# Four-layer graph network on one core: layer two's spread turns its quads through two PSUM banks, two ahead of the weighing, and keeps the scan's mask in SBUF

## Chip, cores and metric

One Trainium2 chip, one core. The metric is the device time of one execution in microseconds (us), outside the profiler; of the kernel before there are three runs.

## What is computed

Four message-passing layers over a graph with 12,500 nodes of 32 features and 400,000 edges sorted by their target; after each comes a residual and a layer norm. The change is in the second layer:

```
bu, bv = tent(edge_attr[:, 0], 4), tent(edge_attr[:, 1], 4)     # hat functions on 4 centres
basis = (bu[:, :, None] * bv[:, None, :]).reshape(-1, 16)
xj = x[edge_index[1]]
msg = sum_k basis[:, k:k+1] * (xj @ weight[k])                  # 16 matrices of 32 x 32
out = segment_sum(msg, edge_index[0], num_segments=n_nodes)
x = layernorm(x + out)
```

For this layer the kernel's source node is the one by which the edges are sorted (`edge_index[1]` is dst), so xj is constant over a run of edges, and the sum goes to scattered nodes.

## The kernel before

Edges lie as [128 partitions x 3125]; every edge stage walks them in 125 chunks of T = 25 columns. Chunk 0 is written out, the other 124 run in a loop of 31 turns with four chunks each (k = 1 to 4). The engines are programmed by hand: each has its own instruction list in the order of the code, and waits on semaphores. The stages, in order of time: layer 1 (chunks with gathers by GpSimd, L1957), its ends, **the spread** of layer 2 (`vector_spread`, `tensor_spread`, `scalar_spread`, `gpsimd_spread`, `sync_spread`), the fold of layer 2 (33 chunks), layer 3 (gathers L1979), layer 4 (gathers L1939).

The spread, one chunk c:
- SyncE loads the injected rows (`S1.inj`) and the edge coordinates (`S1.at`), four buffers each.
- ScalarE (`scalar_chunk1`) waits until the scatters of chunk c - 4 have landed (semaphore `sc{s4}`), copies 25 numbers into the payload buffer (L1340), lays out the scan's input (L1349) and the mask `S1.mr` (L1350), makes the tents (L1354, L1357), and then copies seven turned quads from PSUM to SBUF (`S1.xT`, two buffers, L1362).
- VectorE (`vector_chunk1`, 41 instructions) subtracts the centres (L695), carries the last column over (L697), and spreads the node rows over their runs by a scan with the mask (L700). It multiplies the rows by four tents (L665, two instructions, `oA` for columns 0 to 11 and `oB` for 12 to 24). Then five times a one-hot (L564, `row`) and a rank (L677 and L679, `rank`), and seven times a weighted sum (L688 and L691, `mix`), interleaved; seven small instructions (L723 to L734) make the scatter addresses, the last is `adr`.
- TensorE (`tensor_chunk1`) works on quads of four columns: `turn(g)` transposes four 128x128 blocks into a PSUM bank (L1668), `weigh(g)` multiplies the copied transposes by the weights into bank 2 or 3 (L1677), `before(q)` and `behind(q)` are the rank's triangular matmuls into banks 0 and 1 (L1651, L1652). `mix(g)` waits for `weigh(g)`, `rank(q)` for `before(q)`, `behind(q)` for the first half of `rank(q)`.
- GpSimd (`gpsimd_chunk1`) waits for `adr` and issues 25 indirect DMAs of one column each (L1900), which scatter the payload `S1.pay` (four buffers) to `pay_d`. VectorE's `mix(0)` of chunk c writes into the buffer that chunk c - 4 scattered, so VectorE may be up to about three chunks ahead of GpSimd.

Before the change all seven quads turn through one bank, `ps[6]`: `turn(g + 1)` stands behind `weigh(g)`, and has to wait until ScalarE has copied quad g out. The mask lies in PSUM banks 4 and 5 (`psall[:, 2048:2880]`). The scans of layers 1 and 3 (L847, L1009) also take their mask from PSUM; layer 4's scan (L1158) takes it from SBUF, written there by L1468.

Of the kernel before, what the change touches and what calls it, by code (L numbers as in the profile page):

```python
# [10 lines left out]
ACT = mybir.ActivationFunctionType  # L11
# [6 lines left out]
T = 25  # L18
# [24 lines left out]
def nth4(i, k):  # L43

    return i + 1 + k // 4
# [21 lines left out]
def gnn_kernel(nc, x, src, dst, ea2, ea3, ea5, ew, ew1, W0, W1, G2, MU, SG, ROOT, BIAS, w1, b1, w2, b2, out):  # L67

    ctx = ExitStack()
    with ctx:  # L70
        ctx.enter_context(nc.allow_non_contiguous_dma(reason="small strided loads of weights and block heads"))

        def sb(name, shape, dt=F32):
            return ctx.enter_context(nc.sbuf_tensor("s_" + name, shape, dt))
# [6 lines left out]
        def sem(name):  # L81
            if name not in sems:
                sems[name] = ctx.enter_context(nc.semaphore("m_" + name))
            return sems[name]
# [30 lines left out]
        ident = sb("ident", [P, P])  # L115
# [31 lines left out]
        psall = ctx.enter_context(nc.psum_tensor("psall", [P, 4096], F32))  # L147
        ps = [psall[:, 512 * i:512 * i + 512] for i in range(8)]
# [7 lines left out]
        def barrier(e, name):  # L156

            n = barriers[name] = barriers.get(name, 0) + 1
            e.drain().then_inc(sem("bar"), 1)  # L159
            e.wait_ge(sem("bar"), 5 * n)  # L160
            e.sem_inc(idle2 if name == "sync" else idle, 1)
# [17 lines left out]
        cv = Carve()  # L179
        dsti, dstf, q2 = cv(TP, I32), cv(TP), cv(TP)  # L180
        cv = Carve(17900)
# [12 lines left out]
        for layer in (0, 2):  # L194
            cv = Carve(15400 if layer == 0 else 0)
# [4 lines left out]
        cv = Carve(10350)  # L200
# [23 lines left out]
        cv = Carve()  # L224
# [12 lines left out]
        cv = Carve()  # L237
# [4 lines left out]
        S1 = Spread()  # L242
# [12 lines left out]
        S1.adr = [cv(T, U32) for _ in range(4)]  # L255
        S1.pq, S1.pi, S1.pa = cv(T), cv(T, I32), cv(T)
        S1.wt, S1.wl = cv(128), cv(128)
        assert cv.at <= TOP
        S1.tv = ps[7][:, 0:4 * T]
        S1.cen = ps[7][:, 200:204]  # L260
        S1.mr = psall[:, 2048:2048 + 32 * (T + 1)]
        S1.mrv = S1.mr.rearrange("p (f t) -> p f t", f=32)
        QUADS = [(4 * g, 4) for g in range(6)] + [(24, 1)]

# [1 line left out]
        cv = Carve()  # L266
# [19 lines left out]
        cv = Carve()  # L286
# [11 lines left out]
        cv = Carve(21400)  # L298
# [10 lines left out]
        cv = Carve()  # L309
# [22 lines left out]
        cv = Carve()  # L332
# [308 lines left out]
        def v1(c, name):  # L641

            return c * PER1 + (mk["base1"] + ST[name])
# [692 lines left out]
        def scalar_chunk1(e, c, i, k):  # L1336
            i_ = 0 if i is None else i
            s4, s2 = k % 4, k % 2
            e.wait_ge(sem(f"sc{s4}"), (0 if i is None else i * 400) + (416 if k == 4 else 16))
            e.activation(S1.pay[s4].rearrange("p (t c) -> p t c", c=33)[:, :, 32:33], lo[:, bass.ds(c * T, T)].unsqueeze(2), ACT.Copy).then_inc(sem("p1_lo"), 1)  # L1340
            e.wait_ge(sem(f"inj1_{s4}"), nth4(i_, k) * 16)
            e.wait_ge(dv.h, v1(c - 1, "scan"))
            if i is None:


                e.wait_ge(sem("ld_d0"), 16)
                e.activation(S1.siv[0][:, :, 1:2], frow[:, :].unsqueeze(2), ACT.Copy)
            t0 = 1 if i is None else 0
            e.activation(S1.siv[s2][:, :, 1 + t0:T + 1].rearrange("p f t -> p t f"), S1.inj[s4][:, 32 * t0:].rearrange("p (t f) -> p t f", f=32), ACT.Copy)  # L1349
            e.activation(S1.mrv[:, :, 1:T + 1], mask[:, bass.ds(c * T, T)].unsqueeze(1).to_broadcast([P, 32, T]), ACT.Copy).then_inc(sem("p1_si"), 1)  # L1350

            te = S1.tent.rearrange("p (t d m) -> p t d m", t=T, d=2)
            e.wait_ge(dv.h, v1(c, "tent"))
            e.activation(S1.tent, S1.tent, ACT.Abs).then_inc(sem("p1_a"), 1)  # L1354
            e.wait_ge(sem("p1_a"), c + 1)
            for d, o_ in ((1, S1.tv), (0, S1.tu)):
                e.activation(o_.rearrange("p (t m) -> p t m", t=T), te[:, :, d], ACT.Relu, scale=-1.0 / H3C, bias=ones[:, 0:1]).then_inc(sem("p1_b"), 1)  # L1357
            for g, (t0, n) in enumerate(QUADS):
                xb = (k + g) % 2
                e.wait_ge(sem("p1_t"), c * 7 + (g + 8))  # L1360
                e.wait_ge(sem("p1_y"), c * 7 + (g + 1))
                e.activation(S1.xT[xb][:, 0:128 * n], ps[6][:, 0:128 * n], ACT.Copy).then_inc(sem("p1_x"), 1)  # L1362

        def scalar_spread(e):
            e.sem_inc(sem("p1_b"), 2)
            e.sem_inc(sem("p1_si"), 4)
            e.sem_inc(sem("p1_x"), 1)
            e.wait_ge(sem("ld_wt1"), 64)
            e.activation(S1.wt.rearrange("p (o a) -> p o a", a=4), S1.wl.rearrange("p (a o) -> p o a", a=4), ACT.Copy).then_inc(sem("p1_w"), 1)
            barrier(e, "scalar")  # L1370
            scalar_chunk1(e, 0, None, 0)
            with e.Fori(0, 31) as i:
                for k in range(1, 5):
                    scalar_chunk1(e, i * 4 + k, i, k)
# [217 lines left out]
        def scalar_program(e):  # L1592
            scalar_setup(e)
            scalar_table(e, 0)
            scalar_ends(e)
            scalar_edges0(e)
            e.wait_ge(sem("ld_ew"), 32)
            scalar_ends_of(e, 0)
            scalar_spread(e)
            barrier(e, "scalar")  # L1600
            scalar_fold(e)
            scalar_ends_of(e, 1)
            scalar_table(e, 2)
            barrier(e, "scalar")
            scalar_edges2(e)
            scalar_ends_of(e, 2)
            scalar_edges3(e)
            scalar_ends_of(e, 3)
            barrier(e, "scalar")
# [40 lines left out]
        def both(e, lhsT, rhs, start):  # L1650
            e.matmul(R5s[:, 0:4], lhsT, rhs[:, 0:4], start=start, stop=True, skip_group_check=True)  # L1651
            return e.matmul(R5s[:, 4], lhsT, rhs[:, 4], start=start, stop=True, skip_group_check=True)  # L1652
# [8 lines left out]
        def tensor_chunk1(e, c, k):  # L1661
            def turn(g):

                t0, n = QUADS[g]
                e.wait_ge(dv.h, v1(c, "oA" if t0 < 12 else "oB"))
                e.wait_ge(sem("p1_x"), c * 7 + (g + 1))
                for t in range(n):
                    m = e.transpose(ps[6][:, 128 * t:128 * t + 128], S1.xb[:, 128 * (t0 + t):128 * (t0 + t) + 128], ident[:, :])  # L1668
                m.then_inc(sem("p1_t"), 1)

            def weigh(g):
                t0, n = QUADS[g]
                yb = (k + g) % 2
                e.wait_ge(sem("p1_x"), c * 7 + (g + 2))
                e.wait_ge(dv.h, v1(c, f"mx{g - 2}") if g > 1 else v1(c - 1, f"mx{g + 5}"))
                for t in range(n):
                    m = e.matmul(ps[2 + yb][:, 128 * t:128 * t + 128], S1.xT[yb][:, 128 * t:128 * t + 128], S1.wt, start=True, stop=True)  # L1677
                m.then_inc(sem("p1_y"), 1)

            def before(q):  # L1680
                e.wait_ge(dv.h, v1(c, f"oh{q}"))
                both(e, trib, O[q], False).then_inc(sem("rk"), 1)

            def behind(q):
                e.wait_ge(dv.h, v1(c, f"tm{q}"))
                both(e, ntrib, O[q], False).then_inc(sem("rk"), 1)

            turn(0)
            before(0)
            for g in range(4):  # L1690
                weigh(g)
                turn(g + 1)
                behind(g)
                before(g + 1)
            weigh(4)
            turn(5)
            behind(4)
            weigh(5)
            turn(6)
            weigh(6)  # L1700

        def tensor_spread(e):
            e.sem_inc(sem("p1_t"), 7)
            e.sem_inc(sem("p1_y"), 2)
            barrier(e, "tensor")
            e.wait_ge(sem("p1_w"), 1)
            tensor_chunk1(e, 0, 0)
            with e.Fori(0, 31) as i:
                for k in range(1, 5):
                    tensor_chunk1(e, i * 4 + k, k)  # L1710
# [556 lines left out]
```

## Time and profile before

| | us |
|---|---|
| runs of the kernel before | 17419.0, 17419.1, 17439.26 |
| median | 17419.1 |
| span of the profiled execution | 22369.0 |
| layer 1's chunks in it (first to last gather L1957) | 202.2 to 4570.8 |
| the spread in it (first to last scatter L1900) | 4971.7 to 10827.7 |
| layer 3's chunks (L1979) | 11454.7 to 15800.7 |
| layer 4's chunks (L1939) | 15985.0 to 22107.1 |

The page gives no device time of the profiled execution other than its span, and that is 4950 us above the runs without the profiler. So the profile shows well how long single instructions take, while its waits have to be read with care: some of them are in the profiled execution alone. The granted clock is the mean of TensorE's clock, 0.5 being 1.2 GHz and 1.0 being 2.4 GHz.

### The profile page before, as it was taken

Reading aid. Unit: us, or ns where it says so; the run is one execution under the profiler, and the core shown is the slowest. Engines: PE = TensorE matmul, PEld = TensorE weight load, DVE = VectorE, ACT = ScalarE, POOL = GpSimd, SP = SyncE. Lnnn points to the kernel's source line nnn. Section 1 sums busy time; section 2 is a strip of 40 time slices with the busy share of each in tenths; the row PEclk is TensorE's granted clock in tenths of the full one; section 3 lists DMA queues with packets and bytes.
Section 4 is the critical chain, followed back from the end, with each engine's and each line's share of the span. In section 5 each row is a group of like instructions: output and inputs, shape, how many; then the busy total and the mean of one; then the engine's idle time right before and its main releaser. Section 6 shows DMA issues by size and latency. Waiting matters only on the chain. (4 is left out here: it accounts for less than half of the span.)

```text
span 22369.0 us, 139122 instructions
## 1 busy us (share of the span) xinstructions
PE 7326.9 (33%) x33487; PEld 5554.2 (25%) x33487; DVE 12331.2 (55%) x15713; ACT 3280.0 (15%) x5336; POOL 13220.2 (59%) x13715
## 2 busy tenths in 40 slices
PE   1000000014444444444420000000166666666665
PEld 0000000003333333333310000000155555555553
DVE  5566666646666666666742222222366666666665
ACT  0000000001111111111520000000011211211111
POOL 7766666655555555555667777777644444444444
PEclk9555555556666666666655555555588888888887
DMA  3232232210000000000322222222111111111111
GB/s 94 80 89 84 86 89 86 85 36 19 18 19 19 18 19 19 19 19 18 131 92 52 53 52 52 53 52 53 34 35 37 36 35 36 36 35 37 36 35 30
DMA packets 744245, 1076.69 MB, mean 48 GB/s; under 512 B 375704, under 2 KB 508494, under 8 KB 731295
## 3 DMA queue, kind: packets, MB, share of 16 engines
q0 software_dynamic: 417376, 477.82, 9.8%
q1 hardware_dynamic: 250851, 398.14, 6.3%
q10 hardware_dynamic: 75736, 197.70, 2.4%
q8 instruction: 88, 1.44, 0.0%
q14 instruction: 194, 1.58, 0.0%
HBM read 684.92 MB, written 389.48 MB: 48 GB/s over the span
## 5 line engine op out<-in xcount | busy, mean ns | idle before, releaser
L1939 POOL DMA_INDIRECT s_arena<-d_t,s_arena x3125 | 2963.9, 948 | 3178.4 <-DVE s_arena L1091 1107.9
L1900 POOL DMA_INDIRECT d_pay<-s_arena x3125 | 3029.2, 969 | 2873.4 <-DVE s_arena L697 1464.3
L1979 POOL DMA_INDIRECT s_arena<-d_t,s_arena x3125 | 3320.8, 1063 | 1106.6 <-issue 1026.1
L1957 POOL DMA_INDIRECT s_arena<-d_t,s_arena x3125 | 2993.1, 958 | 1405.8 <-issue 1373.3
L1758 PE MATMUL psall<-s_w2r,s_arena 128*128 128x384 f32 x4750 | 2107.2, 580 | 1550.1 <-DVE s_arena L1091 625.2
L1651 PE MATMUL psall<-s_arena 128*128 128x500 bf16 x1875 | 945.5, 559 | 4749.1 <-remote 2889.7
L992 DVE TENSOR_TENSOR s_arena<-s_arena,psall 128x2400 f32<-128x2400 f32 x125 | 332.0, 2656 | 3141.9 <-DMA s_arena<-d_t,s_arena 3141.9
L1677 PE MATMUL psall<-s_arena 128*128 128x128 f32 x6250 | 1356.1, 381 | 1813.2 <-ACT s_arena L1362 1706.9
L1758 PEld LDWEIGHTS psall<-s_w2r,s_arena 128*128 128x128 f32 x4750 | 1447.1, 320 | 1943.0 <-DVE s_arena L1091 687.6
L1677 PEld LDWEIGHTS psall<-s_arena 128*128 128x128 f32 x6250 | 1166.0, 277 | 2111.8 <-issue 1209.9
L1088 DVE TENSOR_TENSOR s_arena<-psall,s_arena 128x512 f32<-128x512 f32 x1000 | 786.7, 787 | 1454.1 <-remote 1161.2
L1651 PEld LDWEIGHTS psall<-s_arena 128*128 128x128 bf16 x1875 | 243.2, 130 | 5164.8 <-remote 2934.6
L901 DVE TENSOR_REDUCE s_arena<-s_arena 128x600 f32<-128x4200 f32 x125 | 1027.2, 8218 | 775.5 <-remote 678.6
L1840 PE MATMUL psall<-s_tails,s_mfix 128*128 128x32 f32 x6 | 1.9, 412 | 4400.9 <-POOLq L159 4374.3
L1100 DVE TENSOR_REDUCE s_arena<-s_arena 128x64 f32<-128x1024 f32 x1000 | 1397.6, 1408 | 0.2 <-issue 0.2
L1362 ACT ACTIVATE s_arena<-psall 128x512 f32<-128x512 f32 x875 | 482.9, 552 | 4807.9 <-remote 2507.1
L1668 PE MATMUL psall<-s_ident,s_arena 128*128 128x128 f32 x3125 | 719.6, 369 | 1274.9 <-DVE s_arena L665 1274.9
L688 DVE TENSOR_TENSOR s_arena<-psall,s_arena 128x512 f32<-128x512 f32 x875 | 550.6, 629 | 1056.2 <-remote 935.3
L1840 PEld LDWEIGHTS psall<-s_tails,s_mfix 128*128 128x128 f32 x6 | 1.5, 313 | 4402.6 <-issue 4374.6
L564 DVE TENSOR_TENSOR s_arena<-s_arena,psall 128x625 bf16<-128x625 f32 x1250 | 962.7, 801 | 132.8 <-issue 132.4
L677 DVE TENSOR_TENSOR s_arena<-s_arena,psall 128x625 f32<-128x625 bf16 x625 | 503.1, 805 | 938.3 <-remote 720.3
L1668 PEld LDWEIGHTS psall<-s_ident,s_arena 128*128 128x128 f32 x3125 | 554.8, 197 | 1298.1 <-issue 1298.1
(303 smaller groups left out, 16992.3 us busy)
## 6 DMA issues: line engine op xcount, KB each, us to landing
s_arena<-d_t,s_arena POOLq DMA_INDIRECT x9375
d_scan<-s_arena ACTq DMA_DIRECT2D x375, 400.0 KB
s_arena<-d_ew SPq DMA_DIRECT2D x126, 800.0 KB
s_arena<-d_pay SPq DMA_DIRECT2D x33, 1650.0 KB, 6.8
d_inj<-s_agg SPq DMA_DIRECT2D x125, 400.0 KB
s_arena<-d_inj SPq DMA_DIRECT2D x125, 400.0 KB
d_pay<-s_arena POOLq DMA_INDIRECT x3125
d_fold<-s_arena ACTq DMA_DIRECT2D x33, 1250.0 KB, 4.9
```

The source lines that it names most:

```text
L564: return e.tensor_tensor(O[sl], h5[:, :, bass.ds(n, 1)].to_broadcast([P, 5, 125]), iob, ALU.is_equal)
L901: e.tensor_reduce(S[:, :, 8:32], w7.rearrange("p m t c -> p t c m"), AX.X, ALU.add)
L1088: e.tensor_tensor(pr[:, :, 0:256].rearrange("p t (b v) -> p t b v", v=16), Rg[:, :, 0:256].rearrange("p t (b v) -> p t b v", v=16), L3.G[s ...
L1100: e.tensor_reduce(L3.sums[s2][:, t0:t0 + n].rearrange("p t c -> p (t c)"), prod(g).rearrange("p t (b v) -> p (t b) v", v=16), AX.X, ALU.ad ...
L1651: e.matmul(R5s[:, 0:4], lhsT, rhs[:, 0:4], start=start, stop=True, skip_group_check=True)
L1668: m = e.transpose(ps[6][:, 128 * t:128 * t + 128], S1.xb[:, 128 * (t0 + t):128 * (t0 + t) + 128], ident[:, :])
L1677: m = e.matmul(ps[2 + yb][:, 128 * t:128 * t + 128], S1.xT[yb][:, 128 * t:128 * t + 128], S1.wt, start=True, stop=True)
L1758: m = e.matmul(ps[BANK[g] + t][:, 0:384], hv_[:, :, t0 + t], L3.w2v if g in ONPE else w2r[:, :], start=True, stop=True)
L1900: e.indirect_dma_start(pay_d, bass.IndirectOffsetOnAxis(ap=S1.adr[s4][:, t:t + 1], axis=0), S1.pay[s4][:, 33 * t:33 * t + 33], None).then_ ...
L1939: e.indirect_dma_start(L3.gb[s][:, t], None, T3_d, bass.IndirectOffsetOnAxis(ap=L3.idx[s][:, t:t + 1], axis=0)).then_inc(sem(f"g3_{s}"), 16)
L1957: e.indirect_dma_start(L0.gb[s][:, t * 128:(t + 1) * 128], None, T0_d, bass.IndirectOffsetOnAxis(ap=L0.idx[s][:, t:t + 1], axis=0)).then_i ...
L1979: e.indirect_dma_start(L2.gb[k][:, t * 96:(t + 1) * 96], None, T2_d, bass.IndirectOffsetOnAxis(ap=L2.idx[k][:, t:t + 1], axis=0)).then_inc ...
```

## The change

The mask `S1.mr` moves from PSUM to SBUF. Banks 4 and 6 become `S1.turn`, and quad g of chunk k turns through bank (k + g) % 2 of them. TensorE turns quads 0 and 1 first, and `turn(g + 2)` stands where `turn(g + 1)` stood. The semaphore `p1_x` starts at 2 in place of 1, so a turn waits for the copy of the quad two before, not of the last one.

```diff
         S1.wt, S1.wl = cv(128), cv(128)
+        S1.mr = cv(32 * (T + 1))
...
-        S1.mr = psall[:, 2048:2048 + 32 * (T + 1)]
+        S1.turn = [ps[4], ps[6]]
...
-                e.activation(S1.xT[xb][:, 0:128 * n], ps[6][:, 0:128 * n], ACT.Copy).then_inc(sem("p1_x"), 1)
+                e.activation(S1.xT[xb][:, 0:128 * n], S1.turn[xb][:, 0:128 * n], ACT.Copy).then_inc(sem("p1_x"), 1)
...
-            e.sem_inc(sem("p1_x"), 1)
+            e.sem_inc(sem("p1_x"), 2)
...
-                    m = e.transpose(ps[6][:, 128 * t:128 * t + 128], S1.xb[:, 128 * (t0 + t):128 * (t0 + t) + 128], ident[:, :])
+                    m = e.transpose(S1.turn[(k + g) % 2][:, 128 * t:128 * t + 128], S1.xb[:, 128 * (t0 + t):128 * (t0 + t) + 128], ident[:, :])
...
-                e.wait_ge(sem("p1_x"), c * 7 + (g + 2))
+                e.wait_ge(sem("p1_x"), c * 7 + (g + 3))
...
             turn(0)
+            turn(1)
             before(0)
             for g in range(4):
                 weigh(g)
-                turn(g + 1)
+                turn(g + 2)
                 behind(g)
                 before(g + 1)
             weigh(4)
-            turn(5)
+            turn(6)
             behind(4)
             weigh(5)
-            turn(6)
             weigh(6)
```

TensorE's list at the beginning of a chunk, before: turn(0), before(0) (two rows), weigh(0), turn(1), behind(0), before(1).

```order
L1668 MATMUL psall<-s_ident,s_arena 128x128 x4
L1651 MATMUL psall<-s_arena 128x4x125
L1652 MATMUL psall<-s_arena 128x125
L1677 MATMUL psall<-s_arena 128x128 x4
L1668 MATMUL psall<-s_ident,s_arena 128x128 x4
L1651 MATMUL psall<-s_arena 128x4x125
```

The same place after the change (all line numbers below the new line 258 are higher by one): the turns of quads 0 and 1 are one block of eight, and the turn behind weigh(0) is that of quad 2.

```order
L1669 MATMUL psall<-s_ident,s_arena 128x128 x8
L1652 MATMUL psall<-s_arena 128x4x125
L1653 MATMUL psall<-s_arena 128x125
L1678 MATMUL psall<-s_arena 128x128 x4
L1669 MATMUL psall<-s_ident,s_arena 128x128 x4
L1652 MATMUL psall<-s_arena 128x4x125
```

One block of four turns moved from behind weigh(0) to ahead of before(0); nothing was added.

TensorE's list at the end of a chunk, before: weigh(4), turn(5), behind(4), weigh(5), turn(6) (one block), and behind it weigh(6).

```order
L1677 MATMUL psall<-s_arena 128x128 x4
L1668 MATMUL psall<-s_ident,s_arena 128x128 x4
L1651 MATMUL psall<-s_arena 128x4x125
L1652 MATMUL psall<-s_arena 128x125
L1677 MATMUL psall<-s_arena 128x128 x4
L1668 MATMUL psall<-s_ident,s_arena 128x128
```

After:

```order
L1678 MATMUL psall<-s_arena 128x128 x4
L1669 MATMUL psall<-s_ident,s_arena 128x128
L1652 MATMUL psall<-s_arena 128x4x125
L1653 MATMUL psall<-s_arena 128x125
L1678 MATMUL psall<-s_arena 128x128 x5
```

The single turn of quad 6 now stands ahead of behind(4), and weigh(5) and weigh(6) follow one another.

## Rows read from the trace of the kernel before

**Rows 1.** The page's busy times: engine, us, share of the span, instructions

```profile
PE 7326.9 (33%) x33487; PEld 5554.2 (25%) x33487; DVE 12331.2 (55%) x15713; ACT 3280.0 (15%) x5336; POOL 13220.2 (59%) x13715
```

**Rows 2.** Lines of GpSimd's gathers and scatters: duration ns min/median/max, first and last start

```profile
L1957 POOL DMA_INDIRECT s_arena<-d_t,s_arena x3125: 938/945/1803, 202.2 to 4570.8; - x196
L1900 POOL DMA_INDIRECT d_pay<-s_arena x3125: 963/970/992, 4971.7 to 10827.7; - x196
L1979 POOL DMA_INDIRECT s_arena<-d_t,s_arena x3125: 940/946/2245, 11454.7 to 15800.7; - x196
L1939 POOL DMA_INDIRECT s_arena<-d_t,s_arena x3125: 938/945/2400, 15985.0 to 22107.1; - x196
```

**Rows 3.** Timeline, the spread's first two chunks: start, duration, engine, line

```profile
4938.44 0.36 DVE L695 TENSOR_TENSOR s_arena<-s_arena,psall 128x200 f32<-128x200 f32 x1 [137.52 <-DMA s_arena<-in_edge_attr]
...
4940.78 1.89 DVE L700 TENSOR_TENSOR_SCAN s_arena<-psall,s_arena 128x832 f32<-128x832 f32 x1 [1.87 <-ACT psall L1350]
...
4970.93 0.36 DVE L695 TENSOR_TENSOR s_arena<-s_arena,psall 128x200 f32<-128x200 f32 x1 [0.16 <-issue]
...
4971.43 1.89 DVE L700 TENSOR_TENSOR_SCAN s_arena<-psall,s_arena 128x832 f32<-128x832 f32 x1
4971.70 0.97 POOL L1900 DMA_INDIRECT d_pay<-s_arena  x1 [45.67 <-DVE s_arena L697]
4972.98 0.97 POOL L1900 DMA_INDIRECT d_pay<-s_arena  x1 [0.30 <-issue]
```

**Rows 4.** What ended VectorE's idle time before L695 (us, times)

```profile
  issue: 89.7, 31
```

**Rows 5.** Timeline of a settled chunk: GpSimd's last scatters, ScalarE and VectorE

```profile
8051.12 0.97 POOL L1900 DMA_INDIRECT d_pay<-s_arena  x1 [0.30 <-issue]
8055.20 0.69 DVE L688 TENSOR_TENSOR s_arena<-psall,s_arena 128x512 f32<-128x512 f32 x1 [7.36 <-remote]
8055.34 0.60 ACT L1362 ACTIVATE s_arena<-psall 128x512 f32<-128x512 f32 x1 [14.21 <-remote]
```

**Rows 6.** Waits in the spread (4940:10830): total us, times, longest

```profile
DVE s_arena L688 <- PE psall L1677: 115.1, 149, 1.7
...
DVE s_arena L677 <- PE psall L1652: 90.6, 259, 0.7
```

**Rows 7.** Timeline in layer 4: scans with an SBUF mask, GpSimd's DMAs beside them

```profile
16447.58 1.88 DVE L1158 TENSOR_TENSOR_SCAN s_arena<-s_arena 128x832 f32<-128x832 f32 x1
16447.91 2.30 POOL L1939 DMA_INDIRECT s_arena<-d_t,s_arena  x1 [14.16 <-DVE s_arena L1100]
...
16450.51 0.94 POOL L1939 DMA_INDIRECT s_arena<-d_t,s_arena  x1 [0.30 <-issue]
...
18614.34 1.88 DVE L1158 TENSOR_TENSOR_SCAN s_arena<-s_arena 128x832 f32<-128x832 f32 x1
18614.58 2.40 POOL L1939 DMA_INDIRECT s_arena<-d_t,s_arena  x1 [14.07 <-DVE s_arena L1100]
...
19011.36 1.88 DVE L1158 TENSOR_TENSOR_SCAN s_arena<-s_arena 128x832 f32<-128x832 f32 x1
19012.19 1.80 POOL L1939 DMA_INDIRECT s_arena<-d_t,s_arena  x1 [14.65 <-DVE s_arena L1100]
```

**Rows 8.** Lines of the three scans and the two mask copies: duration ns min/median/max

```profile
L700 DVE TENSOR_TENSOR_SCAN s_arena<-psall,s_arena x125: 1890/1890/1892, 4940.8 to 10749.2; 128x832 f32<-128x832 f32 x125
L847 DVE TENSOR_TENSOR_SCAN s_arena<-psall,s_arena x125: 1890/1891/1891, 250.0 to 4641.7; 128x832 f32<-128x832 f32 x125
L1158 DVE TENSOR_TENSOR_SCAN s_arena<-s_arena x125: 1874/1880/1893, 16152.2 to 22206.4; 128x832 f32<-128x832 f32 x125
L1350 ACT ACTIVATE psall<-s_mask x125: 925/943/967, 4939.8 to 10747.9; 128x800 f32 x124, 128x800 f32<-128x800 f32 x1
L1468 ACT ACTIVATE s_arena<-s_mask x125: 889/891/927, 16027.9 to 22167.7; 128x800 f32 x120, 128x800 f32<-128x800 f32 x5
```

## The prediction

> **What bounds the kernel now.** I began with the busy times [rows 1]: no engine is busy over 59% of the profiled span, which looks as if waits were the bound. But that span is 22369.0 us and the runs without the profiler take 17419.1. So the first question was which of the waits are real. GpSimd's four lines of indirect DMAs answer it [rows 2]. There are 3125 in each of the four stages. One takes 0.97 us in the spread and 0.945 us in the others, and 0.30 us of issue time stands ahead of each ([rows 3, 7]): steps of 1.27 to 1.28 us and of 1.25 us. If GpSimd never waited, the stages would last 3125 x 1.275 = 3984 us (spread) and 3 x 3125 x 1.25 = 11719 us (the others), 15703 together. In the profile they last, from the first and last starts, 4368.6, 5856.0, 4346.0 and 6122.1, together 20693, so all that lies outside them is 22369 - 20693 = 1676 us. 15703 + 1676 = 17379, 40 us below the median of the runs. That is my main reading: without the profiler the four edge stages run at about the pace at which GpSimd issues indirect DMAs, and most of the other idle time belongs to the profiled execution. It is an estimate: the 1676 us may shrink too without the profiler, which would leave room for a stage or two that is slower than GpSimd.
>
> Two rows show what kind of wait goes away. In a settled chunk VectorE and ScalarE stand still for 7.36 and 14.21 us with a releaser outside the trace, and both go on 3 us after GpSimd's last DMA of the chunk [rows 5]. The spread's first chunk, beside which no scatter runs, has no such pause: its L695 starts at 4938.44, the next one at 4970.93 [rows 3].
>
> **VectorE's own pace in the spread.** That first chunk takes 32.49 us, of which 1.87 us are the start-up wait for the first mask and 0.16 us issue [rows 3]: 30.46 us. At the loop's turn, every fourth chunk, 89.7 / 31 = 2.9 us of issue time come on top [rows 4], 0.72 us per chunk. So VectorE needs 31.2 us a chunk, GpSimd 25 x 1.275 = 31.9 us. GpSimd is the slower of the two by 0.7 us, and VectorE, which may be three chunks ahead, waits for it. The two are close, and this decides the case.
>
> **The change, part by part.**
> 1. *Turning two ahead.* The same 25 transposes, 25 weighings and 7 copies are done; only the order and one wait differ. What it can remove is VectorE's waiting for TensorE: 115.1 us before L688 (mix for weigh) and 90.6 us before L677 (rank for before) in the whole spread [rows 6], together 205.7 us or 1.65 us a chunk. That is the upper bound of the gain. In the undisturbed first chunk nearly none of these waits is there, since the 30.46 us are within 0.3 us of the sum of the steps; the bulk stands behind the profiler's pauses, when all engines start again at once. The lower bound is nothing. While GpSimd sets the pace, both ends are worth 0, because VectorE's 31.2 us are hidden behind GpSimd's 31.9. I take 0. If that cover were gone, it would be 0 to 205.7 us. The new waits add nothing: turn(g + 2) needs the copy of quad g, for which weigh(g), just ahead of it, has waited already.
> 2. *ScalarE's mask copy into SBUF.* L1468 does the same copy into SBUF in 0.891 us, L1350 into PSUM in 0.943 us [rows 8]: 0.05 us less, off the path. 0.
> 3. *The scan's duration.* 1.880 us with the mask in SBUF against 1.890 [rows 8]. 0.
> 4. *What the scan does to GpSimd.* Here lies the cost. L700 and L847 take the mask from PSUM. L700 runs in 124 chunks beside GpSimd's stream, and of 3125 scatters none took over 0.992 us [rows 2]. Layer 4's L1158 takes both inputs from SBUF. Its scan mostly falls where GpSimd pauses, but 14 gathers of layer 4 begin while it runs: eleven of them take 1.80 to 2.40 us in place of 0.945, one 1.03, and they are the only ones of that layer above 1 us; the two that begin in its last 0.15 us take the usual time. The rows show the rule: the scan from 16447.58 ends at 16449.46, the gather that began 0.33 us into it lasts 2.30 us and ends at 16450.21, 0.75 us behind the scan's end; the one from 0.24 us ends at 18616.98 (scan 18616.22), the one from 0.83 us at 19013.99 (scan 19013.24) [rows 7]. Each time 0.75 us are left to do once the scan is over. So about 0.945 - 0.75 = 0.2 us after its start such a DMA reads SBUF, and is held there until a scan with two SBUF inputs has ended. The step to the next one grows by the same amount, with the usual 0.30 us between [rows 7].
>
> The Trainium skill ("SBUF — State Buffer", section "Who interferes with whom") says this of two SBUF inputs: they contend with a GpSimd instruction that reads SBUF, through a shared read interface. The same section holds that a tensor_tensor was not seen to stall DMAs, because descriptor generation needs the write interface (an inference there). By the first the sum gets the term below; by the second it would be 0. The stretched gathers speak for the first.
>
> How much per chunk: the reading points of GpSimd's stream come every 1.275 us, the scan lasts 1.88 us, so one always falls into it, x = 0 to 1.275 us behind its start, and is held for 1.88 - x: 0.6 to 1.88 us, in the middle 1.24. The next one falls behind the scan. Should a DMA instead hold the scan back at its start, the scan only moves later, and VectorE has 0.7 us to spare. The scans of chunks 1 to 124 lie beside the stream: 124 x 1.24 = 154 us (75 to 233 us).
>
> Sum: 0 + 0 + 0 + 154 us. GpSimd's chunk becomes 33.1 us, still above VectorE's 31.2. There is no price below nothing for part 4, since L1900's shortest step is already free of such holding. The durations come from the profiled execution, whose pauses I don't carry over, so I add the sum to the median: 17419.1 + 154 = **17573 us**.
>
> **Rivals.**
> - *The stream isn't held (12%).* The twelve stretched DMAs are gathers, each the first of a burst after more than 14 us of idle; L1900 is a scatter from the middle of a stream. If it isn't held, parts 1 to 4 are 0: 17419 us. Against it: both forms carry offsets in SBUF.
> - *VectorE sets the pace and gains (16%).* For it speaks that GpSimd's step without the profiler is not shown. If it is below the profile's, and TensorE's waits are real, VectorE's chunk goes from 31.2 + 1.65 = 32.85 to 31.2 us at best: 17419 - 206 = 17213 us at the utmost; with the few waits of the first chunk, 0 to 0.3 us, it is 0 to 37 us. To show as a gain, GpSimd's new chunk has to stay below VectorE's old one: 25 s + 1.24 < 31.2, a step s under 1.20 us, or under 1.26 with all of TensorE's waits. This is the case on the other side. The four stages' sum, which fits the runs with the profile's steps, speaks against it.
> - *VectorE sets the pace, and GpSimd takes over (14%).* With the profile's step and TensorE's waits real, the chunk is 32.85 us before and 33.1 after: +0.25 x 124 = 31 us, 17450 us; with half of the waits +1.1 x 124 = 136 us. Half of this case lies within 0.2%.
> - *The forecast: GpSimd sets the pace and is held once a chunk (58%)*: 17494 to 17652 us, the likeliest one's own range.
>
> **How the numbers follow.** 0.2% of the time, 35 us, is about what a measurement of this kernel can tell from no change. Slower by more: the forecast's 58% and 8% of the take-over, 66%. Within 0.2%: 12% of the stream that isn't held, 6% of the take-over, 4% of the small gains, 22%. Faster by more: 12%. The range reaches from 17340 (the larger half of the gains left out, some 8%) to 17665 (a little above the forecast's upper bound).
>
> **What would show it.** In the profile after, in the spread: one of GpSimd's 25 scatters of a chunk, the one beside the scan, takes about 1.6 to 2.8 us where the longest was 0.992, and ends 0.75 us behind the scan; the line's maximum shows it at once. The scan stays at 1.88 us. VectorE's waits for TensorE before L688 and L677 (one line number higher) fall below 205.7 us, and ScalarE's copies come earlier, while the time doesn't follow. The prediction is wrong if L1900's maximum stays below 1 us (then part 4 fails), or if it is stretched and the time falls all the same (then GpSimd was not the pace, and the reading of the four stages fails).

## Result

| | us, median | runs |
|---|---|---|
| before | 17420.13 | 4 (17419.0 to 17439.26) |
| after | 17582.26 | 4 (17577.15 to 17582.94) |

The ratio is 1.0091 (95% interval 1.0079 to 1.0103): 162 us slower, where 154 were forecast.

To read the numbers one has to know that the kernel before takes about 17420 us on some chips, called quick here, and 22389 us on one other, called the slow chip, both without the profiler; whether this belongs to the chip or to its condition at the time, no run tells. By its span of 22369 us the profile of before is of the slow sort, and the one of after is of the quick sort. The two profiles must therefore not be subtracted from each other. The last experiment has a profile of the kernel before on a quick chip, and with this one after is compared. In every experiment with a ratio the runs of before come from the same chip.

The page of after: span, then busy time of each engine as in [rows 1].

```profile
span 17580.9 us, 139122 instructions
...
PE 6286.6 (36%) x33487; PEld 5104.7 (29%) x33487; DVE 12239.2 (70%) x15713; ACT 3270.3 (19%) x5336; POOL 13107.4 (75%) x13715
```

GpSimd's indirect DMAs in after, one line for each stage, which answer to [rows 2]: duration ns min/median/max, first and last start.

```profile
L1958 POOL DMA_INDIRECT s_arena<-d_t,s_arena x3125: 938/944/1026, 204.9 to 4104.6; - x196
L1901 POOL DMA_INDIRECT d_pay<-s_arena x3125: 965/969/2618, 4451.7 to 8591.7; - x196
L1980 POOL DMA_INDIRECT s_arena<-d_t,s_arena x3125: 940/944/1182, 9219.1 to 13131.4; - x196
L1940 POOL DMA_INDIRECT s_arena<-d_t,s_arena x3125: 940/944/2576, 13311.7 to 17360.4; - x196
```

And what ended GpSimd's idle time before the scatters L1901 (us, times):

```profile
  issue: 931.1, 3055
  DVE s_arena L698: 45.7, 1
  DVE s_arena L678: 18.9, 62
```

The longest scatter went from 0.992 us to 2.618. The spread lasts 8591.7 - 4451.7 = 4140.0 us; 3124 steps of the median 1.274 us would be 3980. GpSimd waits once, before its first scatter (45.7 us); all other idle entries are the usual 0.30 us of issue, whatever name stands beside it. The 160 us are inside the scatters: 124 of the 3125, one for each scan but the first, are over 1.05 us.

The timeline of after around two such scans:

```profile
6002.80 0.25 ACT L1341 ACTIVATE s_arena<-s_arena 128x25 f32 x1 [6.75 <-DMA d_pay<-s_arena]
6002.93 1.69 ACT L1350 ACTIVATE s_arena<-s_arena 128x800 f32<-128x800 f32 x1
...
6004.40 0.88 ACT L1351 ACTIVATE s_arena<-s_mask 128x800 f32 x1
...
6005.42 1.89 DVE L701 TENSOR_TENSOR_SCAN s_arena<-s_arena 128x832 f32<-128x832 f32 x1 [3.12 <-ACT s_arena L1351]
...
6005.59 2.50 POOL L1901 DMA_INDIRECT d_pay<-s_arena  x1 [0.30 <-issue]
...
6038.76 1.89 DVE L701 TENSOR_TENSOR_SCAN s_arena<-s_arena 128x832 f32<-128x832 f32 x1 [3.10 <-ACT s_arena L1351]
...
6038.95 2.47 POOL L1901 DMA_INDIRECT d_pay<-s_arena  x1 [0.30 <-issue]
```

The scatter that begins 0.17 us into the scan ends at 6008.09, 0.78 us behind the scan's end (6007.31). The chain reads from the top: ScalarE has waited 6.75 us for the landing of scatters, then lays out the scan's input and the mask; VectorE has waited 3.12 us for them (it waits so before 69 of its 125 scans, 196.3 us in all). So VectorE and ScalarE wait for GpSimd here, not the other way round.

### The profile page after: what moved, and what is told of

It reads as the page before. It is cut to its first block and busy times, and to the rows that moved or that the text cites. A ratio compares the mean times of both kernels' runs of the same rounds, so it can differ in the third digit from the quotient of the medians.

```text
span 17580.9 us, 139122 instructions
## 1 busy us (share of the span) xinstructions
PE 6286.6 (36%) x33487; PEld 5104.7 (29%) x33487; DVE 12239.2 (70%) x15713; ACT 3270.3 (19%) x5336; POOL 13107.4 (75%) x13715
## 5 line engine op out<-in xcount | busy, mean ns | idle before, releaser
L1901 POOL DMA_INDIRECT d_pay<-s_arena x3125 | 3188.9, 1020 | 997.8 <-issue 931.1
L1940 POOL DMA_INDIRECT s_arena<-d_t,s_arena x3125 | 3097.7, 991 | 971.1 <-issue 941.3
L1980 POOL DMA_INDIRECT s_arena<-d_t,s_arena x3125 | 2961.2, 948 | 1032.8 <-issue 952.1
L1958 POOL DMA_INDIRECT s_arena<-d_t,s_arena x3125 | 2948.6, 944 | 982.7 <-issue 952.0
L1652 PE MATMUL psall<-s_arena 128*128 128x500 bf16 x1875 | 834.9, 500 | 4389.3 <-DVE psall L882 3638.0
L1759 PE MATMUL psall<-s_w2r,s_arena 128*128 128x384 f32 x4750 | 1730.4, 495 | 16.1 <-DVE s_arena L1092 5.9
L1669 PE MATMUL psall<-s_ident,s_arena 128*128 128x128 f32 x3125 | 634.9, 345 | 1635.7 <-DVE s_arena L666 1635.7
L1678 PE MATMUL psall<-s_arena 128*128 128x128 f32 x6250 | 1043.2, 315 | 5.5
L1678 PEld LDWEIGHTS psall<-s_arena 128*128 128x128 f32 x6250 | 913.4, 223 | 148.4 <-DVE s_arena L689 51.4
L891 DVE TENSOR_TENSOR s_arena<-s_arena,psall 128x600 f32<-128x600 f32 x125 | 97.5, 780 | 1174.1 <-DMA s_arena<-d_t,s_arena 1174.1
L1515 ACT ACTIVATE s_arena<-s_arena 128x800 f32<-128x800 f32 x125 | 213.8, 1711 | 3491.1 <-DVE psall L865 3461.8
L1089 DVE TENSOR_TENSOR s_arena<-psall,s_arena 128x512 f32<-128x512 f32 x1000 | 785.7, 786 | 37.6 <-PE psall L1759 23.0
```

The source lines that it names most:

```text
L1089: e.tensor_tensor(pr[:, :, 0:256].rearrange("p t (b v) -> p t b v", v=16), Rg[:, :, 0:256].rearrange("p t (b v) -> p t b v", v=16), L3.G[s ...
L1669: m = e.transpose(S1.turn[(k + g) % 2][:, 128 * t:128 * t + 128], S1.xb[:, 128 * (t0 + t):128 * (t0 + t) + 128], ident[:, :])
L1759: m = e.matmul(ps[BANK[g] + t][:, 0:384], hv_[:, :, t0 + t], L3.w2v if g in ONPE else w2r[:, :], start=True, stop=True)
L1901: e.indirect_dma_start(pay_d, bass.IndirectOffsetOnAxis(ap=S1.adr[s4][:, t:t + 1], axis=0), S1.pay[s4][:, 33 * t:33 * t + 33], None).then_ ...
L1940: e.indirect_dma_start(L3.gb[s][:, t], None, T3_d, bass.IndirectOffsetOnAxis(ap=L3.idx[s][:, t:t + 1], axis=0)).then_inc(sem(f"g3_{s}"), 16)
L1958: e.indirect_dma_start(L0.gb[s][:, t * 128:(t + 1) * 128], None, T0_d, bass.IndirectOffsetOnAxis(ap=L0.idx[s][:, t:t + 1], axis=0)).then_i ...
```

## Experiments

Twelve runs. e2_mask_only, e1_mask_psum, e5_halves and e4_extra3 ran on the slow chip, all others on quick ones; so four kernels were run on both.

**e2_mask_only and e2_again: the mask alone.** The kernel before with:

```diff
+        S1.mr = cv(32 * (T + 1))
...
-        S1.mr = psall[:, 2048:2048 + 32 * (T + 1)]
```

> The kernel before with only the mask of layer two's scan moved to SBUF; turning stays as it was, through one bank. Theory H (GpSimd sets the pace, and the scan with two SBUF inputs holds one of its 25 scatters a chunk): the whole loss is in this half, 162 us over before, about 17582 us, with about 124 stretched scatters of 2.2 to 2.6 us. Rival T (the new turning order costs: three turns of the PE list moved, another bank pair): little or none of the 162 us, under 17460 us. If both contribute, something between.

> The kernel before with only the mask in SBUF, as e2_mask_only. On a chip where the kernel before takes 17420 us, theory H: the whole loss is here, 17582 to 17588 us, 124 stretched scatters with 160 to 163 us in all. Rival T (the turning order has a part in the loss): less, by that part; e1_again has already left it little room.

Measured: on the slow chip 22536.1 against 22388.5 us, ratio 1.0066 (1.0049 to 1.0083), +148 us; on a quick chip 17586.6 against 17425.0, 1.0093 (1.0076 to 1.0110), +162 us. The scatter's line on the quick chip:

```profile
L1900 POOL DMA_INDIRECT d_pay<-s_arena x3125: 968/972/2603, 4460.5 to 8612.7; - x196
```

Again 124 stretched scatters, 165 us over their median in all. The whole loss is in the mask.

**e1_mask_psum and e1_again: turning two ahead, mask in PSUM.** Two whole banks are no longer free for the mask, so it is kept for 16 features only and read twice:

```diff
-        S1.mr = cv(32 * (T + 1))
+        S1.mr = ps[5][:, 0:16 * (T + 1)]
...
-            up(e.tensor_tensor_scan(S1.so[s2], S1.mr, S1.si[s2], 0.0, ALU.mult, ALU.add), "scan")
+            for h in range(2):
+                m = e.tensor_tensor_scan(S1.so[s2][:, 416 * h:416 * h + 416], S1.mr, S1.si[s2][:, 416 * h:416 * h + 416], 0.0, ALU.mult, ALU.add)
+            up(m, "scan")
```

> The changed kernel with its turning two ahead, but the mask in PSUM again. Since only one bank is left for it, it holds the mask of 16 of the 32 features, and the scan is made in two halves of 416 that both read it. Theory H: no scatter over 1.0 us, the time of before, 17420 us within 0.2%: nothing is gained by turning ahead, because GpSimd sets the pace. Rival T: about 17580 us, since the order of the turns is kept. Rival V (VectorE had set the pace and turning ahead is worth something that the mask hid): 17215 to 17385 us.

> The same kernel as e1_mask_psum: turning two ahead, a half-size mask in PSUM, the scan in two halves. On a chip where GpSimd's stream sets the pace (17420 us before), theory H: no scatter over 1.0 us, 17420 us within 0.2%, turning ahead gains nothing. Rival V: 17215 to 17385 us. Rival T (the turning order costs by itself): about 17580 us. On the other kind of chip it repeats its 82 us of gain.

Measured: on the slow chip 22306.8 against 22388.5 us, 0.9967 (0.9953 to 0.9981), -82 us; on a quick chip 17418.3 against 17420.4, 0.9999 (0.9990 to 1.0009). There the scatters are as before:

```profile
L1903 POOL DMA_INDIRECT d_pay<-s_arena x3125: 965/970/989, 4455.6 to 8439.8; - x196
```

So on a quick chip the new turning order neither costs nor gives anything; rivals T and V fall. The expectation of 17420 us for the first of the two was made for a quick chip; on the slow one turning ahead, together with the half-size mask, is worth 82 us (below).

**after_again: the change once more.** The changed kernel, beside the same runs of before as e1_again.

> The changed kernel itself, once more beside the kernel before. The first four kernels ran on a chip on which the kernel before takes 22389 us, like its profile (22369 us), and not 17420. Theory H with both parts additive there: mask in SBUF +148 us (e2_mask_only), turning ahead and its share of the mask -82 us (e1_mask_psum), so about +66 us, 22455 us, if this call lands on such a chip; +162 us, 17582 us, on one of the quick kind.

Measured: 17588.2 against 17420.4 us, 1.0096 (1.0079 to 1.0113). Its profile has 124 stretched scatters with 163 us in all. The change as a whole was not run on the slow chip; +66 us there stays an expectation.

**e4_extra3 and e4_again: how much slack VectorE has.** The kernel before, with the reduce of three quads made a second time into scratch:

```diff
+                if g in (1, 2, 3):
+                    e.tensor_reduce(S1.junk.rearrange("p (t o) -> p t o", t=4), w.rearrange("p (t o a) -> p t o a", t=n, a=4), AX.X, ALU.add)
```

> The kernel before with three more VectorE instructions a chunk: the reduce of a weighed quad made a second time into scratch, 0.7 us each, 2.1 us in all (input in SBUF, one only; the output stays the same). Theory H: VectorE's chunk goes from 31.2 to 33.3 us, GpSimd's 31.9 no longer covers it: (33.3 - 31.9) x 124 = 174 us over before, 17594 us. Rival V (VectorE set the pace already): the full 2.1 x 124 = 260 us, 17680 us. If GpSimd had more slack than the profile says, less than 174.

> The kernel before with 2.1 us more of VectorE's work per chunk, as e4_extra3. On a quick chip, theory H: VectorE's chunk 31.1 + 2.1 = 33.2 us against GpSimd's 31.88: 1.35 x 124 = 167 us over before, 17587 us, and GpSimd now waits at the start of chunks. Rival V (VectorE set the pace): 260 us, 17680 us. If VectorE's slack is larger than the 0.75 us that the profile shows: below 17540 us.

Measured: on a quick chip 17562.6 against 17425.0 us, 1.0079 (1.0062 to 1.0096), +138 us; on the slow chip 22452.4 against 22388.5, +64 us. GpSimd's waits on the quick chip:

```profile
POOL d_pay L1903 <- issue: 926.2, 3025, 0.5
...
POOL d_pay L1903 <- DVE s_arena L700: 195.4, 94, 47.9
```

Now it waits for VectorE at 94 chunk starts (L700, named as the releaser, stands just behind the address), and no scatter is stretched. The time is 29 us below the 167 expected, and the trace says why: an added reduce (L693) takes 0.69 us, but the next instruction starts 0.61 us behind its start.

```profile
6026.06 0.69 DVE L693 TENSOR_REDUCE s_arena<-s_arena 128x128 f32<-128x512 f32 x1
...
6026.67 0.68 DVE L694 TENSOR_REDUCE s_arena<-s_arena 128x128 f32<-128x512 f32 x1
```

So three of them add 1.8 us a chunk, not 2.1: VectorE's step from one L698 to the next is 32.94 us, against 31.17 in before_again without its waits for ScalarE. GpSimd's 25 steps of 1.277 us on this chip make 31.92 us. That leaves 1.0 us a chunk to come out, and the stage lasts 4114.3 us where 3124 steps make 3989, 125 us more. Covered were 31.92 - 31.17 = 0.75 us, just the slack of the expectation. Had VectorE set the pace, all of it would have come out, 124 x 1.8 = 223 us. So GpSimd sets the pace before the change, by about 0.75 us a chunk. The remaining 13 of the 138 us lie outside the stage; what they are is not shown.

**e5_halves and e5_again: a shorter hold.** The changed kernel, mask in SBUF, its scan in two halves:

```diff
-            up(e.tensor_tensor_scan(S1.so[s2], S1.mr, S1.si[s2], 0.0, ALU.mult, ALU.add), "scan")
+            for h in range(2):
+                m = e.tensor_tensor_scan(S1.so[s2][:, 416 * h:416 * h + 416], S1.mr[:, 416 * h:416 * h + 416], S1.si[s2][:, 416 * h:416 * h + 416], 0.0, ALU.mult, ALU.add)
+            up(m, "scan")
```

> The changed kernel, mask in SBUF, its scan cut into two halves of 416 (about 0.95 us each in place of 1.89). Theory H with the reading point 0.2 us into a scatter: the first half holds a scatter for at most 0.95 us minus what has passed; behind it the scatter reads first, and the next reading point comes 1.275 us later, beyond the second half. In the changed kernel the held scatter mostly begins 0.1 to 0.2 us into the scan, so it is held about 0.95 - 0.35 = 0.6 us in place of 1.5: 124 x 0.4 to 0.7 us = 50 to 87 us over before, 17470 to 17507 us. If instead both halves run back to back ahead of the waiting scatter, nothing changes: 17580 us.

> The changed kernel with its scan in two halves, mask in SBUF, as e5_halves (there the stretched scatters fell from 135 to 38 us in all). On a quick chip, theory H: the loss falls with them, 17420 + 38 to 50 = 17458 to 17470 us. Rival: the holding is per scan, not per length of scan, so two scans hold as much or more: 17580 us or over.

Measured: on a quick chip 17488.9 against 17425.0 us, 1.0037 (1.0023 to 1.0051), +64 us; on the slow chip 22378.5 against 22388.5, 0.9997 (0.9988 to 1.0007), -10 us where 50 to 87 us more than before were expected (a range made for a quick chip; what turning ahead gains on the slow one, below, is in the -10 us too). The longest scatter and one pair of halves, from the quick chip:

```profile
L1903 POOL DMA_INDIRECT d_pay<-s_arena x3125: 968/972/1764, 4462.0 to 8506.3; - x196
```

```profile
6019.04 1.94 DVE L702 TENSOR_TENSOR_SCAN s_arena<-s_arena 128x416 f32<-128x416 f32 x2
...
6019.76 1.08 POOL L1903 DMA_INDIRECT d_pay<-s_arena  x1 [0.31 <-issue]
...
6021.15 0.97 POOL L1903 DMA_INDIRECT d_pay<-s_arena  x1 [0.30 <-issue]
```

111 scatters are stretched by 56 us in all, against 162. A scatter is held by one half only: this one ends at 6020.84, 0.14 us ahead of the second half's end, so it got on when the first half was over. Of the 111, 84 end 0.78 us behind a first half and 27 behind a second. So the cost goes with the length of one uninterrupted instruction, not with the number of scans. The time is 64 us over before, a little more than the 38 to 50 us expected.

**e7_tt_sbuf: is it the scan, or the two inputs?** The kernel before, mask in PSUM, with one more tensor_tensor of 750 elements a chunk behind the tents, into scratch:

```diff
+            e.tensor_tensor(S1.junk.rearrange("p (s b) -> p s b", s=6), S1.so[s2][:, 0:750].rearrange("p (s b) -> p s b", s=6),
+                            io125[:, 0:125].unsqueeze(1).to_broadcast([P, 6, 125]), ALU.mult)
```

> The kernel before, mask in PSUM, with one more tensor_tensor of 750 elements a chunk behind the tents (about 0.85 us), both inputs in SBUF, result into scratch. Theory H taken as a rule on two SBUF inputs: it holds scatters as a scan does; since it is shorter than a step of 1.275 us only some chunks are hit, those for at most 0.65 us, ending 0.75 us behind the tensor_tensor: 0 to 80 us over before from this and up to 12 us from VectorE's longer chunk, and the line's longest scatter is over 1.1 us. Rival (a tensor_tensor doesn't hold descriptor generation, only the scan does): no scatter over 1.0 us.

Measured: 17484.1 against 17425.0 us, 1.0035 (1.0022 to 1.0047), +59 us. The scatter's line and one of the places:

```profile
L1903 POOL DMA_INDIRECT d_pay<-s_arena x3125: 965/969/1669, 4453.9 to 8491.6; - x196
```

```profile
6029.78 0.92 DVE L707 TENSOR_TENSOR s_arena<-s_arena,s_io 128x750 f32<-128x750 f32 x1
6030.02 1.53 POOL L1903 DMA_INDIRECT d_pay<-s_arena  x1 [0.30 <-issue]
```

111 scatters are stretched, by 59 us in all, each beside this instruction, ending about 0.85 us behind it. A tensor_tensor holds them as a scan does. The same tensor_tensor with its second input in PSUM was not run; but the kernel's own ones of that kind (L564, L665, L677, L688), 0.3 to 3.3 us long, stand beside the stream all the time and no scatter beside them is stretched (before_again).

Layer three of the kernel before holds the same comparison, with gathers. In before_again:

```profile
9064.95 0.93 DVE L946 TENSOR_TENSOR s_arena<-s_arena,s_mug 128x750 f32<-128x750 f32 x1
9065.64 1.06 POOL L1979 DMA_INDIRECT s_arena<-d_t,s_arena  x1 [0.30 <-issue]
```

L946 has two SBUF inputs; the gather that begins near its end takes 1.06 us in place of 0.945 and ends 0.82 us behind it. 65 gathers beside L946, L948 and L965, all with two SBUF inputs, take over 1 us, 1.18 at most: L946 and L948 are met near their ends, and L965 takes only 0.38 us. None does beside L992, a tensor_tensor of 2.66 us with one input in PSUM, nor beside L1001, a reduce of 2.90 us with one input. So neither the kind of the instruction nor its length decides, but the second SBUF input.

The Trainium skill ("SBUF — State Buffer", section "Who interferes with whom") has both rules that the prediction weighed. Its rule on two SBUF inputs agrees with the 162 and 59 us here. Its inference, that a tensor_tensor doesn't stall DMAs because descriptor generation needs the other interface, doesn't hold for these indirect DMAs: 111 scatters are stretched by it. Which part of such a DMA's work is held, no run shows.

**b1_both: a version that beats both.** e1_mask_psum, and layer four's scan in halves. In every profile from a quick chip layer four's gathers are held as well, because its mask has been in SBUF all along.

```diff
-                e.tensor_tensor_scan(L3.sof[p2], L3.mrf[p2], L3.sif[p2], 0.0, ALU.mult, ALU.add).then_inc(dv.up(), 1)
+                for h in range(2):
+                    m = e.tensor_tensor_scan(L3.sof[p2][:, 416 * h:416 * h + 416], L3.mrf[p2][:, 416 * h:416 * h + 416], L3.sif[p2][:, 416 * h:416 * h + 416], 0.0, ALU.mult, ALU.add)
+                m.then_inc(dv.up(), 1)
```

> e1_mask_psum, and in layer four (whose scan has had its mask in SBUF all along) the scan is cut into two halves of 416 too. On a quick chip: the changed kernel's profile has 123 of layer four's gathers stretched by 149 us in all with no other wait of GpSimd in that stage; halves should cut this to 40 to 80 us by the argument of e5_halves: 17420 - (70 to 110) = 17310 to 17350 us. Rival (layer four is set by VectorE or TensorE as much as by GpSimd): 17400 to 17420 us. On the other kind of chip GpSimd waits 2200 us in layer four, so the halves do nothing there: 22307 us, as e1_mask_psum.

Measured: 17355.3 against 17420.4 us, 0.9962 (0.9948 to 0.9976), -65 us (-63 against e1_again on the same chip). Layer four's gathers in e1_again, and then in b1_both:

```profile
L1942 POOL DMA_INDIRECT s_arena<-d_t,s_arena x3125: 940/946/2596, 13164.1 to 17212.7; - x196
```

```profile
L1944 POOL DMA_INDIRECT s_arena<-d_t,s_arena x3125: 938/944/1746, 13150.2 to 17110.3; - x196
```

The stage shrinks from 4048.6 to 3960.1 us, 88.5 us; of these, 22 us come back after the last gather (span minus its start: 220.9 us, then 243.2). The stretched gathers lose more than that, 104 us in all (142.9 us over their median, then 38.6), but GpSimd now waits for VectorE now and then (L1094: 21 times, 24.2 us). The time is neither in the range expected (17310 to 17350 us) nor in the rival's, by 5 us to the first: the gathers do get through, and then VectorE and the work behind the stage are late.

**before_again: the kernel before on a quick chip.**

> The kernel before, for its profile on a quick chip, which is not there yet. Theory H: the spread lasts 3980 to 3990 us between its first and last scatter, GpSimd waits nowhere in it but before the first, no scatter takes over 1.0 us; VectorE waits for ScalarE, and ScalarE for the landing of the scatters of four chunks before, 0.8 to 1.1 us a chunk; the pauses of VectorE and ScalarE that the first profile shows are gone.

Measured: 17429.2 us, with the profile. The scatter's line and the waits in the spread:

```profile
L1900 POOL DMA_INDIRECT d_pay<-s_arena x3125: 965/970/986, 4455.3 to 8436.0; - x196
```

```profile
PE psall L1677 <- ACT s_arena L1362: 102.2, 250, 0.5
...
DVE s_arena L677 <- PE psall L1652: 21.6, 124, 0.2
```

and what ended VectorE's idle time before its scan L700:

```profile
  ACT psall L1350: 26.7, 25
```

The stage is 3980.7 us, 3124 steps of 1.274 us: GpSimd never waits after its first scatter. The long pauses of [rows 5] are gone. One expectation missed: VectorE waits for ScalarE only 25 times, 26.7 us in all, and not 0.8 to 1.1 us a chunk. It is quicker than GpSimd by so little (31.36 us between two L695 against 31.86 us a chunk) that it needs most of the stage to get its three chunks ahead; but for the first chunk, it waits only from chunk 92 on.

## Why the prediction was right, step by step

- *GpSimd's issue of indirect DMAs sets the pace of the four edge stages.* Right. On a quick chip they last 3901, 3981, 3913 and 4049 us in the kernel before; the steps alone give 3902, 3980, 3902 and 3902. The sum of 15703 us was 142 us too low, nearly all of it in layer four, where the prediction had the stretched gathers in its rows and didn't count them. That the total, 17379 us, still came within 40 us of the runs was in part luck: the 1676 us outside the four stages were read from the slow profile and are 17427 - 15845 = 1582 us on a quick chip, 94 us less.
- *The idle time in [rows 5] belongs to the profiled execution.* Wrong as it was put, and harmless to the sum. It comes with the slow chip: there the runs without the profiler take 22389 us too. The right conclusion, that the timed runs don't have these pauses, followed from the wrong cause.
- *VectorE needs 31.2 us a chunk, GpSimd 31.9.* Right: 31.86 us for GpSimd; VectorE between two L695 takes 31.36 us with 0.19 us of waiting for ScalarE, 31.17 without. e4_again confirms the slack: about 0.75 us a chunk are covered.
- *Turning two ahead is worth 0 while GpSimd sets the pace.* Right (e1_again: 0.9999). It does what it says: TensorE's waiting for the copies, 102.2 us in before_again, is absent from the waits of after and of e1_again. VectorE's wait for TensorE before L677 is 21.6 us in before_again and 21.7 in after, so most of the 205.7 us of [rows 6] was indeed no wait of a quick chip.
- *Mask copy and scan duration: 0.* Right: the copy takes 0.878 us, 0.943 before; the scan 1.891 us, 1.890 before.
- *One scatter a chunk is held until the scan has ended, 1.24 us on average.* Right in its kind, 124 of 124, and the size was off by little: 162 / 124 = 1.31 us. That it was off by so little is partly luck, for the meeting place isn't spread evenly over a step, as the 1.24 us assumed. In after the scan is released by the landing of scatters once VectorE is three chunks ahead, so it meets the stream at the same place in most chunks: 81 of the 124 held scatters are the fourth of their chunk, mostly 0.1 to 0.2 us into the scan, and are held for 1.54 us on average; the other 43 for 0.88 us.
- *Rivals.* The stream is held (after). VectorE doesn't set the pace (e4_again, e1_again). GpSimd doesn't take over from VectorE; it had the pace before.

On the slow chip VectorE and ScalarE pause while GpSimd's stream runs, and go on 3 us after its last DMA [rows 5]. There the chunk is longer than the stream, so one would expect longer scatters to be hidden. They weren't: e2_mask_only's are stretched by 135 us in all, and the time is up by 148. That fits pauses that end with the stream; why the engines pause there was not tested. TensorE's waits are real there: VectorE's waits for it were 205.7 us [rows 6], and in e1_mask_psum they are 98.2 (mix for weigh, rank for before):

```profile
DVE s_arena L689 <- PE psall L1680: 51.3, 41, 2.6
...
DVE s_arena L678 <- PE psall L1655: 46.9, 134, 1.5
```

The difference, 107 us, is of the order of the 82 us gained. So turning ahead probably pays there, but e1_mask_psum also halves the mask copy and cuts the scan, and the parts were not separated.

## What to carry to other kernels

Where GpSimd's stream of indirect DMAs sets the pace, look at every VectorE instruction with two SBUF inputs beside it: each that is longer than a step of the stream (1.27 us here) holds one DMA, for up to its own length, and a shorter one of 0.93 us still held one in 111 of 124 chunks. Keep one input in PSUM; where that can't be, cut the instruction into pieces shorter than the step, which lessens the cost (162 us to 64 here) and doesn't end it. A change that frees a PSUM bank by moving such an input to SBUF is paid for on another engine than the one it is meant to help. And before reading idle time as the profiler's, see whether the timed runs on the profile's chip take as long as the profile.

## What the runs showed of the hardware

- VectorE keeps its time and GpSimd pays: the scan beside the stream takes 1.89 us in 117 of 125 cases and at most 1.95, while a scatter goes to 2.62 us. Held DMAs end 0.75 us (gathers) to 0.78 us (scatters) behind a scan, and 0.82 us (gathers, L946) to 0.85 us (scatters, e7_tt_sbuf) behind a tensor_tensor.
- Two halves of 416 take 1.94 us together, a scan of 832 takes 1.89: cutting costs VectorE 0.05 us.
- A VectorE instruction's duration is more than it adds: the reduces of 0.69 us in e4_again stand 0.61 us apart from what follows.
- One and the same program takes 17420 or 22389 us by the chip, with the same durations of VectorE's and ScalarE's larger instructions in the spread. What differs in the profiles of before and before_again is pauses of these engines beside GpSimd's stream; in layer three 1155 gathers that take over 1 us (367 us over the median in all, against 11 us in before_again); and TensorE, whose granted clock in the spread is 0.64 against 0.76, with a median of 0.421 against 0.273 us for a transpose (L1668). Which of these is a cause is not shown.
